# Wide attention: one maxima instruction for two heads where an item's PSUM banks are neighbours

## The reference

```python
q = query @ w_q                       # 1024 x 1024
k, v = jnp.split(context @ w_kv, 2, axis=-1)   # 6404 x 1024 each
q = q.reshape(B, NQ, 16, 64).transpose(0, 2, 1, 3)
k = k.reshape(B, NKV, 16, 64).transpose(0, 2, 1, 3)
v = v.reshape(B, NKV, 16, 64).transpose(0, 2, 1, 3)
scores = jnp.einsum('bhqd,bhkd->bhqk', q, k) * 64 ** -0.5
attn = jax.nn.softmax(scores, axis=-1)
out = jnp.einsum('bhqk,bhkd->bhqd', attn, v)
```

## Time and profile before

| | us |
|---|---|
| Runs of the kernel before, median of 3 | 3855.21 (3840.88 to 3857.26) |
| Span of the profiled execution, first to last instruction | 3852.1 |
| TensorE's matmuls busy in it | 3585.8 (93%) |
| VectorE busy | 2721.2 (71%) |
| ScalarE busy | 2164.0 (56%) |
| GpSimd busy | 2367.2 (61%) |

### The profile page before, as it was taken

How to read it: one execution, slowest core, us unless ns; L and a number is a source line. 1 busy time by engine, 2 the same in 40 slices (tenths; PEclk the granted TensorE clock), 3 DMA queues, 4 the chain that set the end, 5 groups by cost and what they waited for, 6 DMA issues and landing times.

```text
span 3852.1 us, 61024 instructions
## 1 busy us (share of the span) xinstructions
PE 3585.8 (93%) x23264; PEld 1471.9 (38%) x23264; DVE 2721.2 (71%) x4447; ACT 2164.0 (56%) x2535; POOL 2367.2 (61%) x1280
## 2 busy tenths in 40 slices
PE   6868999999999999889999999999999999999999
PEld 2332222222222244334444444444444444444444
DVE  5758888888888547776766666667666676666742
ACT  4667888888888744644444444444444444444422
POOL 3115656566565303047888888888788888889810
PEclk7969999999999999999999999999999999999999
DMA  4220001010001002500111000101010010012100
GB/s 132 52 44 8 1 10 27 1 26 11 1 1 43 10 5 87 204 14 25 29 29 29 27 28 27 30 25 32 26 29 27 28 29 28 25 55 71 30 0 6
DMA packets 74058, 126.73 MB, mean 33 GB/s; under 512 B 9875, under 2 KB 26341, under 8 KB 73093
## 3 DMA queue, kind: packets, MB, share of 16 engines
q1 hardware_dynamic: 73772, 122.82, 11.2%
HBM read 88.15 MB, written 34.64 MB: 32 GB/s over the span
## 4 chain that ended last, share of the span: by engine, by line
PE 51%; DVE 4%; ACT 2%; issue 1%; DVEq 0%; ACTq 0%
PE PS L2371 20%; PE PS L2345 12%; PE PS L2300 6%; PE PS L2358 5%; PE PS L2318 3%; DVE att_top_piece L2555 2%; DVE att_k_lo L2569 2%; PE PS L340 1%; PE PS L348 1%; PE PS L341 1%; ACT att_k_hi L2463 1%; PE PS L2311 0%; PE PS L2329 0%; PE PS L2323 0%; DVE att_prob L2535 0%
## 5 line engine op out<-in xcount | busy, mean ns | idle before, releaser
L2220 POOL TENSOR_TENSOR att_total<-att_total,att_prob 128x1024 f32<-128x1024 f32 x597 | 1543.7, 2586 | 352.4 <-ACT att_prob L2484 304.5
L2484 ACT ACTIVATE att_prob<-PS 128x1024 f32<-128x1024 f32 x816 | 790.9, 1021 | 1005.1 <-PE PS L2358 1005.1
L2555 DVE TENSOR_REDUCE att_top_piece<-PS 128x1 f32<-128x512 f32 (+1 forms) x1560 | 971.8, 664 | 349.6 <-PE PS L2300 339.8
L1878 DVE TENSOR_REDUCE att_top_piece<-PS 128x1 f32<-128x512 f32 (+1 forms) x1459 | 904.9, 664 | 132.4 <-PE PS L1591 127.0
L1781 ACT ACTIVATE att_prob<-PS 128x1024 f32<-128x1024 f32 (+2 forms) x912 | 892.0, 1004 | 173.5 <-PE PS L1623 170.6
L2371 PE MATMUL PS<-att_prob,att_vals 128*64 128x512 f32 x3264 | 792.0, 605 | 3.7 <-issue 2.9
L1646 PE MATMUL PS<-att_prob,cross_Vst 128*32 128x256 f32 (+1 forms) x5544 | 506.5, 431 | 2.7 <-issue 0.8
L1493 POOL TENSOR_TENSOR att_stage<-att_stage,att_run 128x512 f32<-128x512 f32 x150 | 191.4, 1276 | 401.9 <-ACT att_stage L1760 401.6
L2300 PE MATMUL PS<-att_k_hi,att_q_hi 64*128 64x512 f32 (+1 forms) x1664 | 376.3, 449 | 60.3 <-DVE att_top_piece L2555 47.0
L1591 PE MATMUL PS<-cross_Kstack,cross_Qmax 49*128 49x512 bf16 (+1 forms) x1664 | 323.5, 386 | 95.1 <-DVE att_top_piece L1878 33.4
L2345 PE MATMUL PS<-att_q_hi,att_k_hi 64*128 64x512 f32 x1632 | 329.1, 396 | 0.0
(11 more groups left out here) (316 smaller groups left out, 3394.6 us busy)
## 6 DMA issues: line engine op xcount, KB each, us to landing
att_vals<-values SPq DMA_DIRECT2D x192, 256.0 KB, 2.6
values<-att_prob SPq DMA_DIRECT2D x14, 1024.0 KB, 4.1
values<-cross_Vall SPq DMA_DIRECT2D x10, 1024.0 KB, 4.2
cross_Kstack<-kparts SPq DMA_DIRECT2D x36, 204.0 KB
f_w<-in_f_w SPq DMA_DIRECT2D x24, 256.0 KB, 3.7
kparts<-cross_Vst SPq DMA_DIRECT2D x24, 128.0 KB, 1.8
att_vals<-values SPq DMA_DIRECT2D x16, 192.0 KB, 2.3
k_ctxT<-in_ctxT SPq DMA_DIRECT2D x1, 2448.0 KB
```

Source lines behind the costliest of these rows:

```text
L1878: dve.tensor_reduce(top_piece[:, n % 2, s * QT + qt, c:c + 1], PS[:, banks[item][s], 0:w], AX, ALU.max).then_inc(dve_freed, 1)
L2220: pool.tensor_tensor(so_far, so_far, prob[0:rows, j % RING, :, :], ALU.add).then_inc(summed, 1)
L2484: act.activation(prob[:, j % RING, :, :].rearrange("p a b -> p (a b)"), PSf[:, b:b + 2 * HALF], ACT.Exp, scale=scale).then_inc(exped, 1)
L2555: dve.tensor_reduce(top_piece[:, n % 2, s * QT + qt, c:c + 1], PS[:, bank_of(item, s), 0:w], AX, ALU.max).then_inc(dve_freed, 1)
```

## The change

A function adjacent tells whether an item's second bank is its first plus one. For every m item that VectorE reduces straight from PSUM and that is adjacent, one instruction now reduces both banks (128x2 out of 128x2x512) and adds 2 to dve_freed; an item in banks 7 and 5 keeps its two instructions. In unit 0 all of these items were taken in one instruction already and still are. The counts that TensorE waits for are unchanged.

```diff
--- before.py
+++ after.py
@@ -2092,6 +2092,9 @@
 
     def bank_of(item, s=0):
         return first_bank[item] + s if item in first_bank else SIDE + (place[item] + s) % BANKS
+
+    def adjacent(item):
+        return bank_of(item, 1) == bank_of(item, 0) + 1
 
     def value_slot(n, f):
         return (n * VF + f) % VBUFS
@@ -2546,13 +2549,12 @@
                     c, qt = item[2:]
                     w = min(HALF, NCTX - c * HALF)
                     dve.wait_ge(side_filled, filled_count[item])
-                    if item in first_bank:
-
-                        b = first_bank[item]
-                        dve.tensor_reduce(top_piece[:, 0, :, :].rearrange("p (s t) c -> p s t c", s=2)[:, :, qt, c],
-                                          PS[:, b:b + 2, 0:w], AX, ALU.max).then_inc(dve_freed, 2)
-                    for s in range(0 if item in first_bank else 2):
-                        dve.tensor_reduce(top_piece[:, n % 2, s * QT + qt, c:c + 1], PS[:, bank_of(item, s), 0:w], AX,
+                    pieces = top_piece[:, n % 2, :, :].rearrange("p (s t) c -> p s t c", s=2)
+                    if adjacent(item):
+                        b = bank_of(item)
+                        dve.tensor_reduce(pieces[:, :, qt, c], PS[:, b:b + 2, 0:w], AX, ALU.max).then_inc(dve_freed, 2)
+                    for s in range(0 if adjacent(item) else 2):
+                        dve.tensor_reduce(pieces[:, s, qt, c:c + 1], PS[:, bank_of(item, s), 0:w], AX,
                                           ALU.max).then_inc(dve_freed, 1)
                     if (c, qt) == (MF - 1, QT - 1):
                         dve.wait_ge(dve_freed, dve_count[item + (1,)])
```

## The result

The changed kernel takes 3962.98 us (median of 4 runs, 3956.99 to 3973.74) against 3856.24 us (median of 4) for the kernel before: a ratio of 1.0281, 95% interval 1.0258 to 1.0304, so about 107 us slower (99 to 117). The profiled execution's span went from 3852.1 to 3955.3 us.

A forecast was written before the change was run, and what follows sets the result against it. TensorE was taken to bound the kernel, waiting on first-bank releases; 45.0 + 37.3 + 4.0 + 1.0 + 8.1 = 95.4 us on 3855.2 gave 3951 us, range 3905 to 3980.

The forecast's parts named there:

- What bounds the kernel, and which bank counts: Wide attention: TensorE paces; its early fill waits for the preceding late item's first bank, freed 0.53 us later if neighbouring.
- VectorE's own time off the path: Merged maxima save VectorE 0.07 us a pair, 36 us in all, costed at nothing because VectorE idles waiting for TensorE.
- Rounds behind k and q: Late maxima behind a k or q item: early fill already waits, so 69 rounds cost 0.54 us each, 37.3 us.
- y: Late maxima behind a y item: 9 rounds cost 0.45 us each, 4.0 us.
- Two late items in a row: A second late item filled straight behind a neighbouring first one: 15 fills wait 0.54 us more each, 8.1 us.
- Ordinary rounds: Full-width rounds not behind k, q or y items: 150 go from T 0.55 to 0.85, 0.30 us each, 45.0 us.
- T = lateness + 0.58: T: last score matmul to first subtraction; lateness: first bank's release minus that matmul's start; formula applies to late releases.
- Short chunk: Early fills behind a late item of the 260-key last chunk: 19 rounds cost 0.05 us each, 1.0 us.
- only existing waits growing: Rival: ordinary rounds have slack, so only waits already there grow; +50 us, 3906 us, chance 0.07.
- slack swallowed the waits: Rival: slack elsewhere in the round, ScalarE's or GpSimd's, absorbs the added waits; 3855 us, chance 0.03.
- The backlog theory: Rival: TensorE's fill waits for VectorE's whole backlog, so shorter work makes it faster; 3819 us, chance 0.03.
- that rival: Rival: TensorE's gaps lower its clock to 0.91 over 1870 us, another 170 us; about 4120 us, chance 0.04.

The follow-up runs named there:

- e1: The kernel before, still two instructions an item, but where its banks are neighbours the second bank is reduced first: 3968.96 us, ratio 1.0287.
- e2: The changed kernel with one instruction only for neighbouring early items; late items keep two: 3856.84 us, ratio 1.0003 to the kernel before.
- e3: The changed kernel with one instruction only for neighbouring late items; early items keep two: 3956.68 us, ratio 1.0255 to the kernel before.
- e8: The kernel before, neighbouring early items reduced by one instruction: one output from both banks, or two from the first bank's halves; 3875.67 us.
- e9: The changed kernel, its two-bank instruction adding 1 to the semaphore instead of 2, wait counts matched: 3954.22 us, ratio 1.0249 to the kernel before.
- e4: The kernel before, with TensorE's early fill moved behind the subtraction of the maxima: 3976.13 us, ratio 1.0309.
- e11: e4 with VectorE's additions cut to one column a head: 3878.07 us, ratio 1.0055 to the kernel before.
- e12: The kernel before with VectorE's additions cut to one column a head: 3853.05 us, ratio 0.9998.

## Why the prediction was right

- **What bounds the kernel, and which bank counts:** held. e1 moves nothing but the moment at which the first bank is freed, and has the whole loss; e2 and e3 put it on the late items, as the plan of the ring said.
- **VectorE's own time off the path:** held. It saved 34 us (36 were reckoned) and e2 shows that half of this is worth nothing. On the rule weighed there, 125 ns an instruction: the trace stays with 0.07 a pair.
- **Rounds behind k and q, 37.3 us:** measured 37.3, T 1.64 against the 1.65 reckoned. **y:** 4.1 against 4.0. **Two late items in a row:** 8.0 against 8.1, of 14 fills and not 15.
- **Ordinary rounds, 45.0 us:** measured 54.1 with the short ones. This is the term that was too small. The formula, T = lateness + 0.58, was right: lateness is 3640.54 + 1.23 - 3641.43 = +0.34, T 0.92. What failed is the clause "the reduction starts when it did": it starts 0.07 us later, because an addition of 2 puts its wait into an instruction of its own (e8, e9). In e9 T is 0.85, the value of the prediction. In k rounds VectorE is busy when the fill ends, so the late start does not show there.
- **Short chunk, 1.0 us:** of 20 such rounds 19 cost nothing, though their lateness went from -0.53 to -0.18 (medians). The prediction took an early release to lower T, and the traces show another reason: T is 0.44 where the early fill itself has only 260 columns (15 of the 19, before and after) and 0.54 in the 4 where it has 512. So up to a lateness of -0.18 the release does not count at all.
- **Rivals:** only existing waits growing (3906) would have left ordinary rounds at 0.55; they went to 0.91. No slack swallowed the waits (3855). The backlog theory wanted the fill to follow VectorE's whole work; e1 and e2 exclude it. The clock stayed at 1.00; the price of that rival was reckoned too low, since at 0.91 the work of 1870 us takes 1870 / 0.91 - 1870 = 185 us more and not 170, which changes no conclusion.

The sum of 95.4 us stands against 109.2 in the stage: 8 more in the ordinary and short rounds (54.1 against 46.0), and 5 to 6 in places that the prediction put at nothing, 3.3 of them in late fills behind an early item; these stay unexplained. The measured 3963 lies inside the range.

## What to carry to other kernels

Merging two instructions on a consumer saves little when it isn't the bound, and it moves the first release to the end of the long one; ask which of the two results or buffers the bounding engine waits for next, and leave that one an instruction of its own, first in order. Write down, for each kind of round, by how much a release comes before the moment that needs it: that one number, from three or four rows, gave every cost here within a tenth of a microsecond. If the releaser is late because it stands behind a chain through another engine (here k_hi and k_lo), change the order of the consumer's queue before the size of its instructions; that was worth 1.1%.

## What the runs showed of the hardware that had not been expected

- A VectorE reduction that adds 2 to its semaphore starts 0.11 us after what it waits for, one that adds 1 starts 0.04 after; the form of the operands makes no difference (e8, e9).
- VectorE's addition of two SBUF inputs takes 1.21 us when it starts ahead of GpSimd's and 2.9 when it starts 0.5 behind it; two columns alone take 1.7 us then (e4, e11, e12). The Trainium skill (SBUF — State Buffer, Who interferes with whom) says that a VectorE instruction with two SBUF inputs contends with a GpSimd instruction that reads SBUF, and that the order of issue decides which of them is blocked. The traces agree both ways: in e4 the 152 late additions of VectorE each ended 1.08 us after GpSimd's, and in the kernel before 163 additions of GpSimd that began within one of VectorE's took 3.13 us, where undisturbed ones took 2.38 (medians). The time that VectorE lost, 1.5 to 1.6 us, hardly depends on the size of its addition. Moving one fill by 0.54 us was enough to turn the order around.
- A fill matmul on 64 rows starts 0.22 us after the start of the matmul ahead of it when that is a score matmul of the same shape, 0.43 when it is the subtraction on 32 rows, and 0.52 when it is a k matmul on 96 rows or a weighing one on 128 (medians, the kernel before and e4). The Trainium skill (TensorEngine Tiling (Array Packing), Key Properties) says that a change of the tiling mode drains TensorE; the gaps agree in direction, and no run here takes the mode apart from the other things that differ between these matmuls.
